# One projection group of each batch split into two 256-column accumulations, in a decoder-layer kernel on one Trainium2 core

## The reference, cut to what matters

```python
q = (hidden_states @ wq.T).reshape(b, s, N_HEADS, HEAD_DIM).transpose(0, 2, 1, 3)
k = (hidden_states @ wk.T).reshape(b, s, N_KV_HEADS, HEAD_DIM).transpose(0, 2, 1, 3)
v = (hidden_states @ wv.T).reshape(b, s, N_KV_HEADS, HEAD_DIM).transpose(0, 2, 1, 3)
...
q = q * cos[None, None] + _rotate_half(q) * sin[None, None]
k = k * cos[None, None] + _rotate_half(k) * sin[None, None]
```

## Time and profile before

| what | before |
|---|---|
| median of three runs | 1408.07 us |
| span of the profiled execution, first to last instruction | 1404.9 us |
| TensorE matmul busy | 1359.3 us, 97% of the span |
| TensorE weight loads busy | 1058.0 us, 75% |
| VectorE, ScalarE, GpSimd busy | 78%, 66%, 70% |
| matmul instructions, weight loads | 8294, 8294 |
| matmuls of the projection in part 1 (L479) | 2304, 570.7 us busy |
| mean granted TensorE clock | 0.986 |

### The profile page before, as it was taken

How to read it: one execution, slowest core, us unless ns; L and a number is a source line. 1 busy time by engine, 2 the same in 40 slices (tenths; PEclk the granted TensorE clock), 3 DMA queues, 4 the chain that set the end, 5 groups by cost and what they waited for, 6 DMA issues and landing times.

```text
span 1404.9 us, 32306 instructions
## 1 busy us (share of the span) xinstructions
PE 1359.3 (97%) x8294; PEld 1058.0 (75%) x8294; DVE 1094.9 (78%) x3869; ACT 931.8 (66%) x3258; POOL 984.3 (70%) x936
## 2 busy tenths in 40 slices
PE   8999999999999999999986999999999999999995
PEld 6777777777777777777754788888888888888873
DVE  5887887878788787787775678887788877888774
ACT  5888888878788887888884455554555545555443
POOL 4777776777777677777774667766777667776653
PEclk9999999999999999999998999999999999999997
DMA  7354545445453544545478865657656666676751
GB/s 264 96 152 123 159 116 158 128 136 159 114 159 117 155 137 129 159 115 164 124 208 242 181 162 157 166 153 171 157 157 165 156 171 156 160 161 158 157 120 45
DMA packets 108861, 213.03 MB, mean 152 GB/s; under 512 B 26640, under 2 KB 32272, under 8 KB 108816
## 3 DMA queue, kind: packets, MB, share of 16 engines
q1 hardware_dynamic: 108480, 211.73, 56.5%
q10 hardware_dynamic: 336, 0.79, 0.2%
HBM read 131.83 MB, written 34.47 MB: 118 GB/s over the span
## 4 chain that ended last, share of the span: by engine, by line
PE 87%; POOL 3%; DMA 2%; SPq 2%; DVE 2%; issue 2%; ACT 2%; ACTq 0%; DVEq 0%; POOLq 0%
PE wo_ps L479 34%; PE wo_ps L1134 23%; PE conv_ps L1145 9%; PE s_ps L509 5%; PE pv_ps L522 4%; PE ffn_ps L1167 4%; PE ffn_ps L1179 3%; PE ffn_ps L1160 2%; PE turn_ps L498 2%; SPq L320 1%; POOL prods L1488 1%; ACT pexp L767 1%; DMA pt<-in_wqkv 1%; DMA raw<-in_xT 1%; PE turn_ps L488 0%
## 5 line engine op out<-in xcount | busy, mean ns | idle before, releaser
L479 PE MATMUL wo_ps<-weights,halves 128*128 128x512 f32 x2304 | 570.7, 400 | 3.5 <-DVE weights L681 3.5
L479 PEld LDWEIGHTS wo_ps<-weights,halves 128*128 128x128 f32 x2304 | 422.8, 189 | 137.8 <-issue 53.8
L767 ACT ACTIVATE pexp<-sm,smin 128x128 f32<-128x128 f32 x1024 | 398.0, 391 | 99.0 <-DVE smin L618 98.0
L1134 PE MATMUL wo_ps<-weights,halves 128*128 128x512 f32 x1464 | 393.2, 401 | 1.0 <-PEq L143 1.0
L1488 POOL TENSOR_TENSOR prods<-prod,prods 128x512 fp32r<-128x512 f32 x192 | 259.3, 1359 | 131.0 <-ACT prods L1382 126.0
L906 POOL TENSOR_TENSOR pn<-pexp,prec 128x512 f32<-128x512 f32 x256 | 265.4, 1041 | 98.1 <-DVE prec L625 98.1
L1134 PEld LDWEIGHTS wo_ps<-weights,halves 128*128 128x128 f32 x1464 | 267.1, 189 | 58.1 <-issue 1.8
L618 DVE CUSTOM_DVE_ANT_0 sm<-s_ps,mask_t 128x128 f32<-128x128 f32 x1024 | 231.9, 282 | 24.9 <-PE s_ps L509 19.6
L1382 ACT CAST prods<-prod 128x512 fp32r<-128x512 f32 x192 | 118.9, 621 | 165.5 <-DVE prod L1271 127.9
L1271 DVE TENSOR_TENSOR prod<-att,x 128x512 f32<-128x512 f32 x192 | 186.6, 987 | 13.3 <-DMA att<-sim_scratch 8.4
L767 ACT ACTIVATION_READ_ACCUMULATOR pexp<-sm,smin 128x1 f32 x1024 | 193.4, 189 | 0.0
(11 more groups left out here) (103 smaller groups left out, 1636.5 us busy)
## 6 DMA issues: line engine op xcount, KB each, us to landing
att<-sim_scratch SPq DMA_DIRECT2D x192, 252.0 KB
pt<-blocks SPq DMA_DIRECT2D x636, 64.0 KB, 2.0
ctx_t<-in_ctx SPq DMA_DIRECT2D x32, 576.0 KB, 5.2
raw<-in_xT SPq DMA_DIRECT2D x32, 512.0 KB, 3.9
xn<-in_x SPq DMA_DIRECT2D x32, 512.0 KB, 7.6
out<-late SPq DMA_DIRECT2D x32, 512.0 KB, 6.2
ot_scratch<-ot SPq DMA_DIRECT2D x63, 256.0 KB, 2.1
raw<-ot_scratch SPq DMA_DIRECT2D x31, 512.0 KB, 6.8
```

What stands on the lines that cost most here:

```text
L479: mm = pe.matmul(qkv_ps[(par + g) % 2][:], xs[:, par, xl, k], w_sb[:, wl, g, k], start=(k == 0 and n == 0), stop=(k == KT - 1 and n == 2))
L767: ins = nc.scalar.activation(pexp[:, c % 2, i * P:(i + 1) * P], sm[:, c % 2, i * P:(i + 1) * P], ACT.Exp, bias=smin[:, c % 2, i:i + 1], sc ...
L1134: mm = pe.matmul(wo_ps[n][:], os_t[:, par, ol, k], wo_sb[:, wl, k, n * BANK:(n + 1) * BANK], start=(k == 0 and m == 0), stop=(k == KT - 1 ...
```

## The change

For every batch but the first, group 0 runs its 24 matmuls of 512 columns as 48 of 256 columns. Slots 0 to 3 accumulate the key columns (0 to 255) over all eight slices, two slices in each slot, and slots 4 to 7 the value columns (256 to 511). Each half has its own start and stop flags, both in the same bank. `qkv_done` is still raised once, at the last matmul of slot 7, and `rotate` still waits for it. Groups 1 and 2 and batch 0 stay as they were.

```diff
-            for n, (xl, wl) in enumerate(((0, 0), (0, 1), (1, 0))):
-                mm = pe.matmul(qkv_ps[(par + g) % 2][:], xs[:, par, xl, k], w_sb[:, wl, g, k],
-                               start=(k == 0 and n == 0), stop=(k == KT - 1 and n == 2))
+            bank = qkv_ps[(par + g) % 2]
+            if g == 0 and not at_step(t, 0):
+                part, first = divmod(k * 2, KT)
+                cols = slice(part * KV, (part + 1) * KV)
+                for kk in (first, first + 1):
+                    for n, (xl, wl) in enumerate(((0, 0), (0, 1), (1, 0))):
+                        mm = pe.matmul(bank[:, cols], xs[:, par, xl, kk], w_sb[:, wl, 0, kk, cols],
+                                       start=(kk == 0 and n == 0), stop=(kk == KT - 1 and n == 2))
+            else:
+                for n, (xl, wl) in enumerate(((0, 0), (0, 1), (1, 0))):
+                    mm = pe.matmul(bank[:], xs[:, par, xl, k], w_sb[:, wl, g, k],
+                                   start=(k == 0 and n == 0), stop=(k == KT - 1 and n == 2))
             if k == KT - 1:
                 mm.then_inc(qkv_done, 1)
```

## The result

| what | before | with the change |
|---|---|---|
| median of the runs | 1408.72 us (4 runs) | 1417.49 us (4 runs) |
| span of the profiled execution | 1404.9 us | 1414.7 us |
| time of the profiled execution | not shown separately | 1416.78 us |
| matmul instructions | 8294 | 9038 |

The change makes the kernel slower by 8.8 us: ratio 1.0063 with a 95% interval of 1.0049 to 1.0076. Timed once more in a later comparison it was 1415.33 against 1409.02 us, 6.3 us slower, ratio 1.0047 (1.0031 to 1.0064). Of the runs further down, one of the kernel with loads of 112 columns took 1931.19 us at a mean granted clock of 0.652, where all others had 0.985 or more; it is left out of the medians.

The account below looks back on a forecast made before the run. TensorE's matmul pace alone was taken to bound part 1. Pace +2.0 us, weight loads 0 and waits 0, against the runs' median of 1408.07 us, gave 1410.1 us; range 1405.5 to 1420.0 us.

Parts of the forecast that it names:

- Part (1): Projection in part 1: 744 matmuls of 512 columns become 1488 of 256, at 114.9 ns each, costing +2.0 us.
- s: Pace in ns of one 256-column matmul of the projection, taken as 114.9 between bounds of 109.5 and 120.5.
- rival B: Projection's 48 short matmuls a batch each pay the fixed 13.8 ns: pace 120.5 ns, +10.3 us, 1418.4 us; chance 0.28.
- argument for proportion: Projection matmuls: 2.7 ns fixed, the remaining time in proportion to columns, giving 114.9 ns for 256 columns.
- Part (2): Projection's 744 added weight loads: each needs about 107 ns, hidden under the matmul ahead at 114.9 ns; cost 0.
- slack of 8 ns: Time left to a weight load under a 256-column projection matmul, against 120 ns at 512 columns.
- a duration near 284 ns: Sign of rival B at L484, the projection's 256-column matmuls; the forecast expected 278 ns there.
- Rival D: Weight loads set the projection's pace: +24 us at 130 ns, +112 us at 189 ns; chance 0.03.
- Rival C: Short projection streams escape the slower supply: pace 109.5 ns, -6.0 us, 1402.1 us; chance 0.09.
- Part (3): Slots and `qkv_done` in part 1: nothing moves, the signal still comes after slot 7, no gain; cost 0.
- L600's idle time before group 0 stays none: Sign at VectorE's rotation of group 0: it starts without idle time before it, as in the unchanged kernel.
- three rows for proportion: Projection evidence: no extra time at half clock, 166 ns behind the stream in durations, 497 ns after an exposed load.

## Why the prediction was right or wrong

**What bounds the kernel.** Right. The cost is the pace: 0.27 us a batch on TensorE and 8.4 us in total, and the busy time of no other engine grew by as much as 1 us.

**Part (1), the pace of 256 columns.** This step failed. The forecast took s = 114.9 ns; measured is 120.0, so the term is 744 x (240.0 - 227.1) = +9.6 us instead of +2.0. The forecast of 1410.1 us is 7.4 us short of 1417.49. That the time lies inside the range is luck as far as the mechanism goes: the range was drawn up to rival B, whose fixed price the runs refute.

The argument for proportion wasn't empty: with 64, 80 or 112 stationary columns, 256 columns do run at 113 to 113.5 ns. What was wrong is that the pace was asked of the stream alone.

**Part (2), the weight loads at no cost.** This is where the missing 5 ns were. "A load needs about 107 ns of its port and 114.9 ns are there" took the 107 ns from a load with no matmul under way (the two loads start 109 ns apart in the trace) and the overlap from a half-rate stream (L1167), and set both against the slot of a full-rate one. The rows were the nearest ones and still showed another case. The slack of 8 ns that the text named wasn't there: with 128 stationary columns s is 120.0 ns, with 112 it is 113.4. That a load of 128 columns ends too late beside the full-rate stream is the nearest reading of this, and it isn't shown: 96 columns at 116 ns and 116 at 120.0 don't follow from it.

**Rival B** has the right sum (120.5 ns, 1418.4 us) for a wrong reason. Its sign came true, a duration near 284 ns (283 measured), and so couldn't tell it from what is behind the pace. A fixed price of each matmul would not go away with fewer stationary columns. **Rival D** is nearest to what the runs showed, in that the pace hangs on the loads, and had chance 0.03, with a price of 24 us and more; measured it is 120 ns and not 130 or more. L1167's pace of 116 ns with a full load was a lower end for it, and the text didn't take that end. **Rival C** (109.5 ns) is out: no stretch with 256 columns was under 113.

**Part (3), waits and signals.** Right in that nothing was gained. The sign "L600's idle time before group 0 stays none" didn't come true: VectorE now waits 0.31 us for group 0, a consequence of the slower pace, which costs nothing by itself.

**The chances.** Slower had 0.41, no change 0.50. The three rows for proportion, all indirect, were given too much weight against a gap in the trace that no row covered: no narrow float32r matmul beside a full load.

## What to carry to other kernels

Cutting a matmul into narrower ones doubles the weight loads, and these aren't free by themselves. With 128 columns of float32 to load, 512 columns of float32r gained nothing from a shorter load, 256 columns ran at 120.0 instead of 113.4 ns, and 224 or fewer waited for the load at 111 to 112 ns. Whether a load fits under a stream has to be read from a place where the stream beside it runs at the same rate. And a partial result is worth its price only if someone is told of it: here the only signal stayed at the end.

## What the runs showed of the hardware that was not expected

- A float32r stream of 512 columns takes 227 ns in group 0 (231 by the medians of groups 1 and 2). 227 is 1/16 over one column in a cycle of the 2.4 GHz level, and 256 columns with 64, 80 or 112 stationary columns take 113.4 ns, with the same 1/16. At the 1.2 GHz level it is gone (426.7 ns), and for plain float32 it is 2.5 ns for 256 columns.
- With 128 stationary columns the same 256 columns take 120.0 ns, though matmuls of 224 columns and fewer follow each other every 111 to 112 ns, each with a load of 128 columns. The Trainium skill ("TensorE: Matmul & The Clock Gate", Step-by-step) says that weights are loaded through a read port of their own and take no read bandwidth from the running matmul. At 512 columns the runs agree with it: loads of 32 and 64 columns left the pace at 230 to 231 ns. For 256 columns they show only that the pace hangs on the number of stationary columns; whether the load slows the stream or ends too late for the next matmul they don't show.
- Why 96 stationary columns take 116 ns and 116 take 120.0, when 112 take 113.4 and 120 take 117, stays open, and so do the 2 to 5 ns over proportion at 288 to 448 columns. The same widths in the same group, and a full load with fewer rows of output, weren't tried.
